# An adaptive-norm block with a mixture of experts on one core: block 6's slots ahead of block 7's normalization, an earlier choice for block 7, and a reordered hand-over to the table-driven tiles

## The reference, cut to what matters

```python
x = L0_attn_x                                   # (2, 2048, 256) f32
h = _layernorm(x) * (1 + ca) + sa
x = x + ga * _L0_attn_ref(h, ...)               # gated linear recurrence over s, then a SiLU-gated product (F = 768)
h = _layernorm(x) * (1 + cb) + sb
x = x + gb * _L0_ffn_ref(h, ...)                # the experts

def _L0_ffn_ref(x, router_w, w1, v1, w2, bias): # D = 256, F = 704, E = 8, TOP_K = 2
    scores = softmax(xt @ router_w)
    expert_weights, expert_idx = top_k(scores, TOP_K)
    h = gelu(xt @ w1[e]) * (xt @ v1[e])
    y = h @ w2[e]
    out = sum(expert_weights * y[expert_idx]) + bias
```

## Time and profile before

| | us |
|---|---|
| median of 3 runs | 848.93 |
| lowest and highest of them | 848.23, 850.63 |
| the profiled execution, its own time | 848.34 |
| its span in the trace | 846.2 |

### The profile page before, as it was taken

One profiled execution on the slowest core, in us unless ns is written; L12 is line 12 of the kernel. 1 busy time (PEld: TensorE's weight loads), 2 busy tenths in 40 slices (PEclk: granted clock), 3 DMA queues, 4 the chain that ended last, 5 costly groups with the idle time before them and its releaser, 6 DMA issues.

```text
span 846.2 us, 18804 instructions
## 1 busy us (share of the span) xinstructions
PE 818.6 (97%) x5006; PEld 724.6 (86%) x5007; DVE 557.7 (66%) x1534; ACT 367.9 (43%) x681; POOL 485.8 (57%) x454
## 2 busy tenths in 40 slices
PE   8899999999999999978999999999999999999995
PEld 4679898988889879757999999999999999999994
DVE  6788777878876848775555655555655565565553
ACT  5884657565564525534224234224233242342221
POOL 2353645868685877569645646537537465383332
PEclk9999999999999999999999999999999999999998
DMA  8141050303021172327532432523324322222221
GB/s 281 34 113 50 2 181 9 119 26 102 14 90 45 58 233 62 142 78 199 153 47 40 137 45 37 150 44 113 68 38 137 51 37 44 38 38 38 38 45 25
DMA packets 49983, 67.64 MB, mean 80 GB/s; under 512 B 4944, under 2 KB 44240, under 8 KB 49936
## 3 DMA queue, kind: packets, MB, share of 16 engines
q1 hardware_dynamic: 36272, 47.71, 18.4%
q0 software_dynamic: 13664, 19.35, 12.2%
HBM read 43.51 MB, written 23.54 MB: 79 GB/s over the span
## 4 chain that ended last, share of the span: by engine, by line
PE 87%; POOL 3%; DVE 3%; issue 1%; ACT 1%; DMA 1%; another core or an unknown queue 0%; ACTq 0%; DVEq 0%; POOLq 0%
PE ps L614 24%; PE ps L616 24%; PE ps L615 24%; PE ps L776 5%; PE ps L742 2%; PE ps L715 1%; POOL routed L2009 1%; DMA out_rows<-y_moe,tok_moe 1%; PE ps L819 1%; PE ps L818 1%; PE ps L660 1%; PE ps L702 1%; PE ps L632 1%; PE ps L667 1%; POOL out_rows L2031 1%
## 5 line engine op out<-in xcount | busy, mean ns | idle before, releaser
L614 PE MATMUL ps<-split,xT_moe_hi 128*128 (+2 forms) x426 | 165.5, 388 | 0.1
L616 PE MATMUL ps<-split,xT_moe_hi 128*128 (+2 forms) x426 | 160.1, 376 | 0.0
L615 PE MATMUL ps<-split,xT_moe_lo 128*128 (+2 forms) x426 | 159.8, 375 | 0.0
L2021 POOL TENSOR_TENSOR y_moe<-y_moe 128x256 f32<-128x256 f32 x69 | 65.9, 956 | 122.8 <-DVE y_moe L1653 122.6
L1174 ACT ACTIVATE hidT_hi<-ps 128x768 fp32r<-128x768 f32 x70 | 56.9, 813 | 177.7 <-PE ps L776 168.6
L2031 POOL DMA_INDIRECT out_rows<-y_moe,tok_moe x71 | 111.1, 1564 | 28.9 <-issue 22.5
L1168 ACT ACTIVATE gelu_moe<-ps 128x704 f32<-128x704 f32 x71 | 53.8, 758 | 133.6 <-PE ps L616 126.9
L614 PE MATMUL ps<-split,hidT_hi 128*128 (+1 forms) x355 | 99.9, 281 | 1.3 <-DVE y_moe L1653 0.7
L615 PE MATMUL ps<-split,hidT_lo 128*128 (+1 forms) x355 | 100.1, 282 | 0.0
L616 PE MATMUL ps<-split,hidT_hi 128*128 (+1 forms) x355 | 99.9, 281 | 0.0
L1970 POOL TENSOR_TENSOR hid_lo<-hf_sb,hid_hi 128x512 fp32r<-128x512 f32 x48 | 67.1, 1399 | 50.8 <-ACT hid_hi L1146 50.7
(11 more groups left out here) (232 smaller groups left out, 1993.9 us busy)
## 6 DMA issues: line engine op xcount, KB each, us to landing
raw<-in_w SPq DMA_DIRECT2D x9, 1408.0 KB
x_moe<-routed SPq DMA_DIRECT2D x74, 132.5 KB
raw<-in_w SPq DMA_DIRECT2D x9, 640.0 KB
x_again<-in_x SPq DMA_DIRECT2D x8, 512.0 KB
out_rows<-x_again SPq DMA_DIRECT2D x8, 512.0 KB
x_sb<-in_x SPq DMA_DIRECT2D x7, 512.0 KB, 3.9
gu_raw<-in_gu_t SPq DMA_DIRECT2D x1, 1536.0 KB, 8.9
raw<-in_w SPq DMA_DIRECT2D x18, 64.0 KB
```

The costliest lines, as they stand in the source:

```text
L614: pe.matmul(dst, a_hi, b_hi, start=first, stop=False)
L615: pe.matmul(dst, a_lo, b_hi, start=False, stop=False)
L616: return pe.matmul(dst, a_hi, b_lo, start=False, stop=last)
L2021: g.tensor_tensor(y_moe[:, t.slot, 0, :], y_moe[:, t.slot, 0, :], y_moe[:, t.slot, 1, :], ALU.add)\
```

## The change

In the hand-written part between block 7 and `tile_step`:

- On DVE `slots(6)` and `weigh(6)` move from behind `norm2_scale(7)` to right behind `norm2_stats(7)`, ahead of `multiply(Tile(1))`. `gate_y(0)` and `count(6)` go behind `hidT_rest(1)`, `count(7)` behind `hidT_rest(2)`, `take_gates(2)` behind `gate_y(1)`. `table` goes behind `multiply(3)` and `xT_rest(4)`; the three `split_lo` of expert 0 go behind `multiply(4)`, one of them behind `take_gates(4)`.
- On TensorE `rank_tokens(6)` moves ahead of `second_product(0)`, `rank_tokens(7)` ahead of `hid_transposes(2)`, `table_transposes` between the two pieces of `first_products(4)`. Six fills with 27 products are replaced by two with 13. `hid_transposes(4)` and `second_product(4)` leave `tile_step(5)` and stand ahead of `x_transposes(5)`.
- On ACT `router_exp(6)` moves ahead of `gelu(1)`, the first two `split_hi` of expert 0 ahead of `hidT_split(1)`, `gelu(2)` between the two copies of block 7, `hidT_split(4)` ahead of `xT_split(5)`.
- On POOL `result_base(6)` moves from ahead of `scatter(5, 0)` to between the second and third quarter of `scatter(6)`.

```diff
--- before.py
+++ after.py
@@ -822,13 +822,15 @@
 
             def tile_step(t):
                 e = entry(pe, TAB_EXPERT, t, E - 1)
-                hid_transposes(t.near(-1))
-                if t.n > EARLY and not final(t):
-                    x_transposes(t.near(1))
+                if t.n > EARLY:
+                    hid_transposes(t.near(-1))
+                    if not final(t):
+                        x_transposes(t.near(1))
                 first_products(t, e)
                 if t.n == EARLY:
                     x_transposes(t.near(1))
-                second_product(t.near(-1), PICKED if t.n == EARLY else pe.snap(kept, min_val=0, max_val=E - 1))
+                else:
+                    second_product(t.near(-1), pe.snap(kept, min_val=0, max_val=E - 1))
                 pe.reg_mov(kept, e)
 
             def count_early():
@@ -991,38 +993,35 @@
             hid_transposes(Tile(0))
             first_products(Tile(1), PICKED, AB[:2])
             first_products(Tile(1), PICKED, AB[2:])
-            pe.wait_ge(gelu_r, 2)
-            fill(0, 3)
+            rank_tokens(6)
             x_transposes(Tile(2))
             second_product(Tile(0), PICKED)
-            rank_tokens(6)
+            pe.wait_ge(gelu_r, 2)
+            fill(0, 8)
             hid_transposes(Tile(1))
             first_products(Tile(2), PICKED, AB[:2])
-            pe.wait_ge(hid_r, 2)
-            fill(2, 4)
             h2_transposes(7, 0)
             first_products(Tile(2), PICKED, AB[2:])
             h2_transposes(7, 1)
+            x_transposes(Tile(3))
             router_logits(7)
-            x_transposes(Tile(3))
             second_product(Tile(1), PICKED)
-            fill(RING, 5)
+            rank_tokens(7)
             hid_transposes(Tile(2))
-            rank_tokens(7)
             first_products(Tile(3), PICKED, AB[:2])
+            first_products(Tile(3), PICKED, AB[2:])
             count_all()
-            first_products(Tile(3), PICKED, AB[2:])
-            fill(RING, 4)
+            x_transposes(Tile(4))
             second_product(Tile(2), PICKED)
-            x_transposes(Tile(4))
-            fill(RING, 4)
-            table_transposes()
-            pe.wait_ge(gelu_r, 4)
-            fill(0, 7)
             hid_transposes(Tile(3))
             first_products(Tile(4), PICKED, AB[:2])
+            table_transposes()
             first_products(Tile(4), PICKED, AB[2:])
             second_product(Tile(3), PICKED)
+            hid_transposes(Tile(4))
+            second_product(Tile(4), PICKED)
+            pe.wait_ge(gelu_r, 5)
+            fill(0, 5)
             x_transposes(Tile(5))
 
             tiles(pe, tile_step)
@@ -1339,25 +1338,25 @@
             h2_copy(6, 1)
             xT_split(Tile(1))
             hidT_split(Tile(0))
+            router_exp(6)
             gelu(Tile(1))
             xT_split(Tile(2))
-            router_exp(6)
-            hidT_split(Tile(1))
             split_hi(act, 0, 0)
             split_hi(act, 0, 1)
+            hidT_split(Tile(1))
             h2_copy(7, 0)
+            gelu(Tile(2))
             h2_copy(7, 1)
-            gelu(Tile(2))
             xT_split(Tile(3))
+            split_hi(act, 0, 2)
             router_exp(7)
-            split_hi(act, 0, 2)
             hidT_split(Tile(2))
             gelu(Tile(3))
             xT_split(Tile(4))
             hidT_split(Tile(3))
             gelu(Tile(4))
+            hidT_split(Tile(4))
             xT_split(Tile(5))
-            hidT_split(Tile(4))
 
             tiles(act, tile_step)
 
@@ -1897,39 +1896,39 @@
             choose(6)
             hidT_rest(Tile(0))
             norm2_stats(7)
+            slots(6)
+            weigh(6)
             multiply(Tile(1))
             xT_rest(Tile(2))
             norm2_centre(7)
             norm2_scale(7)
-            slots(6)
-            weigh(6)
+            hidT_rest(Tile(1))
             gate_y(Tile(0))
             count(6)
-            hidT_rest(Tile(1))
             multiply(Tile(2))
             choose(7)
-            count(7)
             xT_rest(Tile(3))
-            take_gates(Tile(2), expert)
             slots(7)
             weigh(7)
             hidT_rest(Tile(2))
+            count(7)
             gate_y(Tile(1))
+            take_gates(Tile(2), expert)
+            multiply(Tile(3))
+            xT_rest(Tile(4))
             table()
-            split_lo(v, 0, 2)
-            xT_rest(Tile(4))
-            multiply(Tile(3))
-            split_lo(v, 0, 0)
-            table_out()
             hidT_rest(Tile(3))
             gate_y(Tile(2))
-            split_lo(v, 0, 1)
+            table_out()
             multiply(Tile(4))
-            xT_rest(Tile(5))
+            split_lo(v, 0, 0)
             take_gates(Tile(3), expert)
             gate_y(Tile(3))
+            hidT_rest(Tile(4))
+            split_lo(v, 0, 1)
+            xT_rest(Tile(5))
             take_gates(Tile(4), expert)
-            hidT_rest(Tile(4))
+            split_lo(v, 0, 2)
             take_gates(Tile(5))
 
             tiles(v, tile_step)
@@ -2114,7 +2113,6 @@
             hidden_lo(7, 4)
             hidden_lo(7, 5)
             norm2_rstd(6)
-            result_base(6)
             scatter(5, 0)
             scatter(5, 1)
             scatter(5, 2)
@@ -2123,6 +2121,7 @@
             norm2_rstd(7)
             scatter(6, 0)
             scatter(6, 1)
+            result_base(6)
             scatter(6, 2)
             scatter(6, 3)
             scatter(7, 0)
```

## The result

| | us |
|---|---|
| changed kernel, median of 4 runs (lowest, highest) | 857.35 (856.53, 858.42) |
| kernel before beside it, median of 4 | 849.78 (848.23, 850.80) |
| ratio, 95% interval | 1.0095, 1.0074 to 1.0116 |
| the profiled execution of the changed kernel: time, span | 857.91, 855.9 |

The account below looks back on a forecast made before the run. TensorE bounds the kernel: 7.79 us of waits and 2.98 of fills removed, less 5.45 of new waits, give 5.3 us; 848.34 - 5.3 = 843.0, median 843.6. Own bounds 842.4 to 845.0 (56 in 100); range 841.3 to 848.6.

Parts of the forecast that it names:

- the 4.18 us: DVE idle ahead of slots(7), no releaser known; some 3.3 us of it were to go, slots(7) coming 4.5 us sooner.
- The rival of the late signal: At the ranks of block 7 a late signal stays, or additions bind: 2 to 3.5 us lost, 845.6 to 847.1; 18 in 100.
- (a): New TensorE wait ahead of second_product(4), behind hid_transposes(4), for bare splits and DVE's work in front: 2.4 us.
- the clock: Rival: TensorE's granted clock falls with longer waits and fewer fills; 5 us at the lower level cost 2.5, 846.1; 9 in 100.
- mark of scatter 6: POOL's start of block 6's scatter after the earlier slots(6): 350.4 us, 4.7 us sooner than before.
- mark of scatter 7: POOL's start of block 7's scatter, at the later of POOL free and weigh(7) done: near 364.6 us.
- x_transposes(5), no DMA as releaser: Tile 5's transposes on TensorE near 383.2 us, after its rows at 380.1 to 381.6, so TensorE's own work decides.
- (b): New TensorE wait from x_transposes(5) to first_products(5), for the bare split or loading the table's value: 1.0 us.
- (c): New TensorE wait ahead of hid_transposes(5), behind first_products(5), for multiply's pieces and the handing over: 0.95 us.
- hid_transposes of tile 6: Their start on TensorE, which moves the kernel's end by as much: near 396.8 us instead of 402.09.
- the ranks: rank_tokens(7) on TensorE waits for the choice of block 7: up to 0.8 us, taken as 0.6.
- The slower rival: Expert 1's weights and block 6's base delay scatter 7 and tile 5's rows; at 11 us late 852; 7 in 100.

Follow-up runs that it names:

- the move of the base: The kernel before with only result_base(6) moved to the middle of block 6's scatters: 855.52 us, 1.0094 (late); 844.02 us, 1.0004 (punctual).
- late: Sessions (the result's too) whose every trace has 16 to 25 TensorE signals behind their products' end; the kernel before takes 848.4 to 850.4 us there.
- punctual: Sessions in which no trace has a TensorE signal behind its product's end; the kernel before takes 844.0 and 843.5 us there.
- the tail: The change with hid_transposes(4) and second_product(4) put back in tile_step, without the fill of five: 852.85 us, 1.0054 of the kernel before (late).
- The covered waits: The change with 43 products nobody reads put into three long TensorE waits: 854.01 us, 1.0042 (late); 845.49 us, 1.0021 (punctual).
- the fourth group: A late session beside the kernel before; among its runs the change with block 5's scatters held until block 6's transposes are copied: 863.79 us, 1.0153.

## Why the prediction was wrong

**The step that failed** is the weighing of the 4.18 us for which "the profile knows no releaser". I treated them as one odd wait that the change would mostly remove (3.3 of the 4.5 us by which slots(7) were to come sooner), and wrote of the late signal "nothing else in the trace waits so", at 2 to 3.5 us. The trace had 19 late signals, most of them under cover, while the engine that waits for them had other work. The rival of the late signal was the right mechanism, priced at one place of four: in the result late signals stand behind the waits of 2.73, 2.80 and 5.49 us and behind slots(7), and the new wait (a) measured 5.49 us against my 2.4. That the change exposes them, by taking cover away (tile 4 alone at the end) and by moving the scatters beside other transposes, is my reading; the runs show it for the move of the base (1.0094 late, 1.0004 punctual) and for the tail (1.0054 without it).

The second term that failed is the clock, which I had at 2.5 us. In the result TensorE was at the lower level for 17.0 us between 340 and 400 us (14.7 of them busy), in the trace of before for none. At half speed that is up to 7.4 us, an estimate, against the 5.8 us by which the waits grew (15.05 us below against 8.48 and the 0.73 ahead of block 6's logits in the trace of before). The row of before for the window that stands at 0.88 in the result:

```profile
340.00:412.00 72.00, 63.29 (x399) 53.12 (x400) 51.17 (x183) 29.21 (x38) 54.47 (x48) 1.00 0.43 129
```

**Point by point**, against the change in a punctual group, where its steps can be seen without the disturbance, and against the result:

| step | forecast | punctual | the result |
|---|---|---|---|
| logits of block 6 wait | not named | 0.47 | 2.73 |
| mark of scatter 6 | 350.4 | 348.68 | 354.08 |
| mark of scatter 7 | 364.6 | 364.44 | 370.34 |
| (a) wait ahead of second_product(4) | 2.4 | 2.43 | 5.49 |
| x_transposes(5), no DMA as releaser | 383.2 | 382.88 | 398.11 |
| (b), (c) | 1.0, 0.95 | 1.27, 0.95 | 1.27, 0.95 |
| hid_transposes of tile 6 | 396.8 | 397.00 | 411.90 |
| time against before | 0.9937 | 0.9956 | 1.0095 |

The waits (a) and (c) hold where signals are punctual, (b) is 0.3 us too small. That the times agree as well is partly luck: everything in this trace is 1.6 us sooner than in the trace that I predicted from (the logits of block 6 at 338.52 against 340.13), and I had not forecast that. From these logits to the hid_transposes of tile 6 it took 58.48 us against my 56.67, with 6.8 us at the lower clock that I had not in the sum. Laid beside the punctual trace of before, which has 6.8 us at the lower clock too, these transposes come 3.1 us sooner (397.00 against 400.14), not 5.3. The ratio's interval, 0.9940 to 0.9971, just meets the forecast's own bounds, which were 0.9923 to 0.9954. One bound was wrongly added up besides: with (b) and the ranks at nothing the sum gives 843.6 - 1.6 = 842.0, not 841.3.

In the result, the waits listed from 340 us on are 2.73 + 0.47 + 0.97 + 0.37 + 2.80 + 5.49 + 1.27 + 0.95 = 15.05 us, in the punctual trace 0.47 + 0.47 + 0.34 + 2.43 + 1.27 + 0.95 + 0.18 = 6.11. That is 8.9 of the 15 us between the two traces (411.90 against 397.00). Another 1.45 lie ahead of them (h2_transposes(6) at 338.68 against 337.23).

**The clock** makes most of the rest: 17.0 us at the lower level here, 14.7 of them busy, against 6.8 in the punctual trace, all busy, which is some 4 us at half speed (an estimate from the windows). The granted clock falls to the lower of its two levels, 1.2 GHz, at 342.8, just behind the wait of 2.73 us, and twice more between 383.8 and 397.4, around the 5.49 us. Products of 512 columns that follow each other at 0.43 us show it (those at 346.98, 347.41 and 347.84), as in the fills of the earlier trace rows. But a long wait isn't what it takes: in the punctual trace of the change the clock falls at 341.6 and at 358.6, with no wait over 0.47 us ahead. I gave this rival 9 in 100 and 2.5 us of cost, and took its risk from the longest wait alone. The covered waits show its weight in a late session: 0.4 to 0.5% back, though the change was timed in other sessions. But it isn't a reason to fill waits in general: without its fills the kernel before is no slower in either kind.

The Trainium skill (TensorE: Matmul & The Clock Gate, "What's actually happening") has the throttle as the state that activity releases; by this rule alone, taking fills out costs. The runs agree in the direction of the clock (0.992 to 0.996 with the fills, 0.988 to 0.994 without, in the punctual group), not in the time (0.9984 and 0.9989).

**The 5.49 us** go back to a late signal by a detour: gelu(4) starts 5.3 us behind its products, so multiply(4) is late, and split_lo(0, 0) behind it starts at 385.72, where POOL's result_base(7) runs (385.87, 2.94 us), and takes 4.66 us. In the punctual trace the same split runs at 375.52, ahead of result_base(7) at 382.56, and takes 1.71. gate_y(3) and hidT_rest(4) stand behind it, and the 2.95 us that it takes longer are nearly the 3.06 by which the wait is longer (5.49 against 2.43). POOL in the result, then VectorE and POOL in the punctual trace:

```profile
385.87 2.94 POOL L1989 TENSOR_TENSOR x_again<-x_again,mod 128x1024 f32<-128x1024 f32 x1
```

```profile
375.52 1.71 DVE L404 TENSOR_TENSOR split<-raw,split 128x1408 fp32r<-128x1408 f32 x1
```

```profile
382.56 2.96 POOL L1989 TENSOR_TENSOR x_again<-x_again,mod 128x1024 f32<-128x1024 f32 x1
```

The Trainium skill (SBUF — State Buffer, "Who interferes with whom") has both engines share a port under a lock, which I applied to result_base(6) and to no other; the trace agrees with it here, since 4.66 is the split's own 1.71 and POOL's 2.94 one after the other.

**The slower rival** (scatter 7 stuck behind the expert's weights) didn't happen: SP's load ahead of the base changed nothing, and scatter 7 took 10.5 us.

## What to carry to other kernels

A wait whose releaser the profile can't name is to be chased to its producer's end before it is booked as a gain: if a signal came late once, look for all of them, the ones under cover too, since a change that takes cover away can pay for each. A ratio near 1% from one session may not have a sign: here the same two kernels stood at 1.0095 and 1.0084, and at 0.9956. And times that agree with a forecast are to be laid beside a trace of before from the same session.

No kernel here is the best in both kinds. The change is the best where signals are punctual (840.0), the kernel before without its fills where they are late (849.46 against 850.36, not told from no change).

## What the runs showed of the hardware that was not expected

- TensorE's completion signals can reach the other engines up to 5.3 us behind the product's end in its record (gelu at 383.99 for a product that ends at 378.7), in 16 to 25 places per execution in some sessions and in none in others, for the same instructions. In the late sessions the kernel before takes 4 to 7 us longer. All of them belong to products that end while a block's indirect scatter is issued or just behind; signals that were held up come together (four within 0.18 us), while TensorE's own products keep their pace. The DMA packets of the scatters have the same median time of 0.17 us in both kinds. What makes a session late is open: chip 3 stands under a punctual and a late group. It is open, too, what the recording has to do with it, which loses 63 to 79 steps in every late trace.
- The mean granted clock differs from run to run of one kernel (before: 0.989 to 0.996), and the time follows it only loosely: in the fourth group two of its runs took 849.47 us at 0.996 and 849.41 at 0.991. A wait of 1.49 us left it at the full level in one trace, and in two others it fell with no wait over 0.69 us ahead.
